# An expert-layer kernel: scatters ordered only against other experts' scatters, and an earlier transpose of the next tile's rows

## The reference, cut to what matters

```
x = x + xattn(layernorm(x), ctx, ctx, ...)      # gated linear attention, 8 heads
x = x + ffn(layernorm(x), w12, w3, gate_w)      # 8 experts, each token uses 2

scores = x @ gate_w.T                           # 8 scores for each token
topk_scores, topk_idx = top_k(scores, 2)
probs = softmax(topk_scores)
h1, h2 = split(x @ w12[e].T)                    # 512 + 512 columns, expert e
expert_out[e] = (silu(h1) * h2) @ w3[e].T       # back to 256 columns
y = sum over the 2 chosen experts of probs * expert_out
```

## Time and profile before

| what | us |
|---|---|
| median of 3 runs | 795.19 |
| the three runs | 798.36, 795.19, 791.96 |
| span of the profiled execution | 798.1 |

### The profile page before, as it was taken

The page is one execution under the profiler, slowest core; times in us unless marked ns, Lnnn a source line. Parts: engine busy times, 40 slices in busy tenths (PEclk is TensorE's granted clock), DMA queues, the critical chain, the costliest instruction groups (busy, mean ns, idle before and its releaser), DMA issues.

```text
span 798.1 us, 15053 instructions
## 1 busy us (share of the span) xinstructions
PE 662.9 (83%) x3464; PEld 486.9 (61%) x3481; DVE 463.9 (58%) x940; ACT 316.1 (40%) x704; POOL 405.0 (51%) x470
## 2 busy tenths in 40 slices
PE   3781999999999994136999999999999999999981
PEld 1330566676677663114887777777677777777760
DVE  4663477485367568992676455564555655545541
ACT  3554344353245341003555444444444444434430
POOL 2234254445335331563656666666666666566653
PEclk9996898697589695556999999999999999999995
DMA  8875655355345523401232322223223232232221
GB/s 269 283 252 168 174 146 179 116 178 173 110 133 158 173 77 107 171 7 36 41 54 40 47 47 44 50 40 47 47 42 50 42 47 47 40 47 47 41 40 21
DMA packets 70952, 76.34 MB, mean 96 GB/s; under 512 B 12366, under 2 KB 63060, under 8 KB 70932
## 3 DMA queue, kind: packets, MB, share of 16 engines
q1 hardware_dynamic: 54932, 49.86, 20.2%
q0 software_dynamic: 15712, 25.73, 17.8%
q10 hardware_dynamic: 288, 0.52, 0.2%
HBM read 53.14 MB, written 22.94 MB: 95 GB/s over the span
## 4 chain that ended last, share of the span: by engine, by line
DMA 41%; PE 30%; issue 12%; DVE 8%; POOL 3%; ACT 2%; POOLq 2%; SPq 1%; DVEq 0%; ACTq 0%
DMA out_rows<-ys,ixs 36%; PE bank L1160 8%; PE bank L1174 7%; DMA qT_scratch<-qt 3%; PE bank L1155 3%; PE bank L1157 2%; PE bank L1223 2%; POOL ixs L1076 1%; PE bank L1262 1%; PE bank L1191 1%; PE bank L1264 1%; PE bank L1263 1%; PE bank L1200 1%; DVE ohp L907 1%; DVE wabs L797 1%
## 5 line engine op out<-in xcount | busy, mean ns | idle before, releaser
L1080 POOL DMA_INDIRECT out_rows<-ys,ixs x71 | 159.5, 2246 | 72.5 <-DVE ys L959 61.8
L1262 PE MATMUL bank<-w12l,xh 128*128 x284 | 125.4, 441 | 7.0 <-issue 4.8
L959 DVE TENSOR_SCALAR ys<-bank,pc 128x256 f32<-128x256 f32 x71 | 34.4, 484 | 144.9 <-DMA out_rows<-ys,ixs 140.0
L1264 PE MATMUL bank<-w12h,xh 128*128 x284 | 113.0, 398 | 0.0
L1263 PE MATMUL bank<-w12h,xl 128*128 x284 | 112.8, 397 | 0.0
L965 DVE TENSOR_TENSOR w3l<-w,w3h 128x1024 fp32r<-128x1024 f32 x71 | 87.0, 1226 | 30.8 <-issue 29.8
L1068 POOL DMA_INDIRECT xg<-token_table,ixg x71 | 71.9, 1012 | 58.4 <-POOL ixg L1065 58.4
L1174 PEld LDWEIGHTS bank<-aug,c 128*128 128x128 f32 x512 | 78.2, 219 | 37.6 <-issue 32.8
L765 DVE SCALAR_TENSOR_TENSOR c<-bank,d 128x512 f32<-128x512 f32 x64 | 44.2, 690 | 77.0 <-PE bank L1174 69.2
L624 ACT ACTIVATE sg<-bank 128x512 f32<-128x512 f32 x71 | 42.5, 599 | 115.7 <-PE bank L1264 115.7
L1290 PE MATMUL bank<-w3l,hth 128*128 128x256 f32 x284 | 76.0, 300 | 14.0 <-issue 6.9
(11 more groups left out here) (164 smaller groups left out, 1236.5 us busy)
## 6 DMA issues: line engine op xcount, KB each, us to landing
x<-in_x SPq DMA_DIRECT2D x32, 256.0 KB, 3.0
wst<-in_w12T POOLq DMA_DIRECT2D x26, 256.0 KB, 3.6
aug<-in_ctxv SPq DMA_DIRECT2D x16, 264.0 KB, 3.0
ct<-in_ctxT SPq DMA_DIRECT2D x16, 256.0 KB, 4.5
qT_scratch<-qt SPq DMA_DIRECT2D x16, 256.0 KB, 3.8
kt<-in_ctxT SPq DMA_DIRECT2D x16, 256.0 KB
qbd<-qT_scratch SPq DMA_DIRECT2D x64, 64.0 KB
out_rows<-x SPq DMA_DIRECT2D x16, 256.0 KB, 2.2
```

Source lines behind the costliest of these rows:

```text
L1080: q.indirect_dma_start(out=out, out_offset=bass.IndirectOffsetOnAxis(ap=IXS[i][:, 0:1], axis=0), in_=YS[i][:], in_offset=None, compute_op= ...
L1262: mm(acc, XH[i][:, k, :], wl, start=(k == 0), stop=False)
L1264: ins = mm(acc, XH[i][:, k, :], wh, start=False, stop=(k == NK - 1))
```

## The change

1. **Order of the scatters.** The single semaphore `y_added` becomes two, one for even and one for odd tiles. POOL's `add(j)` waits for ys and for a new semaphore `may_add`. SP raises `may_add` once for each tile, in order: for tile j it first waits for a count of the other parity's `y_added`. The count comes from a table `clear` that DVE works out: 16*max((j-1)//2, 0), which says that scatters up to tile j-3 have landed, plus 16 when tile j has another expert than tile j-1, which says that tile j-1's has landed too. With the two YS buffers, tile j's ys implies that scatter j-2 has landed.
2. **Spare rows.** There are two sets of 128 spare rows, for even and odd tiles, so that two scatters in flight never share one. SP zeroes both (two more DMAs) and loads two small constant tables (two more DMAs, ahead of w3).
3. **Index.** The gather and the scatter read their column of `index` directly; the copies ixg and ixs and their waits go. POOL's expert stage is written out for all 71 tiles, without a loop.
4. **Order on PE and DVE.** On PE `rows(j + 1)` moves ahead of `half_up(1)`; on DVE `low(j + 1)` moves ahead of the product hd.

```
-ROWS = N + P
+ROWS = N + 2 * P
...
-                sp.dma_start(table[N:ROWS, :], zrow[:]).then_inc(zero_out, 16)
-                sp.dma_start(out[N:ROWS, :], zrow[:, 0:E]).then_inc(zero_out, 16)
+                for at in (N, N + P):
+                    sp.dma_start(table[at:at + P, :], zrow[:]).then_inc(zero_out, 16)
+                    sp.dma_start(out[at:at + P, :], zrow[:, 0:E]).then_inc(zero_out, 16)
...
+            sp.dma_start(floor16[:], floors).then_inc(slot_consts, 16)
+            sp.dma_start(spare[:], spares).then_inc(slot_consts, 16)
             sp.wait_ge(w_lo, W2 + B)
...
+            def order(j, o):
+
+                at = sp.value_load(clear[0:1, bass.ds(j, 1)], min_val=16, max_val=16 * TILES)
+                sp.wait_ge(y_added[1 - o], at)
+                sp.sem_inc(may_add, 1)
+
+            sp.wait_ge(clear_ready, 1)
+            sp.sem_inc(may_add, 1)
+            for j in range(1, 3):
+                sp.wait_ge(y_added[1 - j % 2], 16)
+                sp.sem_inc(may_add, 1)
+            order(3, 1)
+            with sp.Fori(2, TILES // 2) as it:
+                for o in range(2):
+                    order(it * 2 + o, o)
+            for j in range(TILES // 2 * 2, TILES):
+                order(j, j % 2)
...
                 st.then(v.tensor_copy(etab[:], count[:]))
+                st.then(v.tensor_tensor(turns[:, 1:], count[:, 1:], count[:, 0:TILES - 1], ALU.not_equal))
+                st.then(v.memset(clear[:, 0:1], 16))
+                dve.wait_ge(slot_consts, 32)
+                v.scalar_tensor_tensor(clear[:, 1:], turns[:, 1:], 16.0, floor16[:, 1:],
+                                       ALU.mult, ALU.add).then_inc(clear_ready, 1)
...
-            st.then(v.tensor_scalar(fil[:], bank[1][:, TILES:2 * TILES], 0.0, io[:, P:P + 1], ALU.is_equal, ALU.mult))
+            st.then(v.scalar_tensor_tensor(fil[:], bank[1][:, TILES:2 * TILES], 0.0, spare[:], ALU.is_equal, ALU.mult))
...
+                if ahead:
+                    low(j + 1, 1 - i)
                 if up:
...
                     v.tensor_tensor(HD[i][:], SG[i][:], bank[2 * i + 1][:], ALU.mult).then_inc(hd_ready, 1)
-                if ahead:
-                    low(j + 1, 1 - i)
...
-                    wait(dve, y_added, 16 * (j - 2))
+                    wait(dve, y_added[o], 8 * (j - 1 - o))
...
+            def gather(j):
+
+                x = j % NX
                 wait(pool, xt_psum, j - NX + 1)
                 wait(pool, pc_ready, j - NX + 1)
-                pool.sem_inc(pool_carrier, 1)
-                q.tensor_copy(IXG[x][:], index[:, bass.ds(j, 1)]).then_inc(ixg_ready, 1)
-                pool.wait_ge(ixg_ready, j + 1)
-                pool.sem_inc(pool_carrier, 1)
                 q.indirect_dma_start(out=XG[x][:], out_offset=None, in_=table,
-                                     in_offset=bass.IndirectOffsetOnAxis(ap=IXG[x][:, 0:1], axis=0)
+                                     in_offset=bass.IndirectOffsetOnAxis(ap=index[:, j:j + 1], axis=0)
                                      ).then_inc(xg_in[x], 16)
...
+            def add(j):
+
+                o = j % 2
                 pool.wait_ge(ys_ready, j + 1)
+                pool.wait_ge(may_add, j + 1)
+                q.indirect_dma_start(out=out, out_offset=bass.IndirectOffsetOnAxis(ap=index[:, j:j + 1], axis=0),
+                                     in_=YS[o][:], in_offset=None, compute_op=ALU.add).then_inc(y_added[o], 16)
...
+            for j in range(TILES + 1):
+                if j + NX - 1 < TILES:
+                    gather(j + NX - 1)
+                if j >= 1:
+                    add(j - 1)
...
+                if ahead:
+                    rows(j + 1, (x + 1) % NX)
                 if up:
                     half_up(1)
-                if ahead:
-                    rows(j + 1, (x + 1) % NX)
```

More of the change, by code:

```diff
@@ L77, in build @@
 def build(nc, x, ctx, ctxv, ctxT, gkq, gkk, gkv, ibias, fbias, onw, w12T, w3T, gateT, ident, identb,
-          maskT, trib, marks, iota, nums, out):
+          maskT, trib, marks, iota, nums, floors, spares, out):
     qT_dram = nc.dram_tensor("qT_scratch", (B, P, NG, S), F32).ap()
@@ L107, in build @@
         tri = sb("tri", [P, 2, P], BF16)
-        io = sb("io", [P, P + 1])
+        io = sb("io", [P, P])
         numbers = sb("numbers", [P, 2 * TOPK * NT])
@@ L112, in build @@
         etab = sb("etab", [P, TILES], I32)
+        clear = sb("clear", [P, TILES], I32)
         index = sb("index", [P, TILES], U32)
@@ L199, in build @@
         OHN = [rt(f"ohn{i}", NI * 2 * TILES, BF16) for i in range(4)]
-        fil, count = rt("fil", TILES), rt("count", TILES)
+        fil, count, turns = rt("fil", TILES), rt("count", TILES), rt("turns", TILES)
+        floor16, spare = rt("floor16", TILES), rt("spare", TILES)
         later = rt("later", TILES * (NE - 1))
@@ L213, in build @@
         PC = [sb(f"pc{i}", [P, 1], on=f) for i in range(NX)]
-        IXG = [sb(f"ixg{i}", [P, 1], U32, on=f) for i in range(NX)]
-        IXS = [sb(f"ixs{i}", [P, 1], U32, on=f) for i in range(2)]
         f.close()
@@ L255, in build @@
         hots_made, hots_ready, inverted, tables = sems("hots_made", "hots_ready", "inverted", "tables")
-        ixg_ready, ixs_ready, y_added = sems("ixg_ready", "ixs_ready", "y_added")
+        clear_ready, may_add, slot_consts = sems("clear_ready", "may_add", "slot_consts")
+        y_added = two("y_added")
         xg_in = [sem(f"xg_in_{i}") for i in range(NX)]
@@ L437, in _ @@
             sp.wait_ge(parts_out, 16 * (1 + PARTS))
-            sp.wait_ge(zero_out, 32)
+            sp.wait_ge(zero_out, 64)
             sp.wait_ge(cols_ready, 1)
@@ L1057, in _ @@
             inversion(pool, number)
-            def gather(j, x):
+            def gather(j):
+                x = j % NX
                 wait(pool, xt_psum, j - NX + 1)
                 wait(pool, pc_ready, j - NX + 1)
-                pool.sem_inc(pool_carrier, 1)
-                q.tensor_copy(IXG[x][:], index[:, bass.ds(j, 1)]).then_inc(ixg_ready, 1)
-                pool.wait_ge(ixg_ready, j + 1)
-                pool.sem_inc(pool_carrier, 1)
                 q.indirect_dma_start(out=XG[x][:], out_offset=None, in_=table,
-                                     in_offset=bass.IndirectOffsetOnAxis(ap=IXG[x][:, 0:1], axis=0)
+                                     in_offset=bass.IndirectOffsetOnAxis(ap=index[:, j:j + 1], axis=0)
                                      ).then_inc(xg_in[x], 16)
[L1072 to L1077, removed]
-                pool.wait_ge(ys_ready, j + 1)
[L1079 to L1088, removed]
+            def add(j):
+                o = j % 2
+                pool.wait_ge(ys_ready, j + 1)
+                pool.wait_ge(may_add, j + 1)
+                q.indirect_dma_start(out=out, out_offset=bass.IndirectOffsetOnAxis(ap=index[:, j:j + 1], axis=0),
+                                     in_=YS[o][:], in_offset=None, compute_op=ALU.add).then_inc(y_added[o], 16)
             pool.wait_ge(tables, 1)
@@ L1094, in _ @@
                 pool.wait_ge(row_out[i], 16 * (B // 2))
[L1095 to L1099, removed]
+            pool.wait_ge(zero_out, 64)
+            for j in range(NX - 1):
+                gather(j)
+            for j in range(TILES + 1):
[3 more added lines that the diff above has]
+                    add(j - 1)
+            for o in range(2):
+                pool.wait_ge(y_added[o], 16 * ((TILES + 1 - o) // 2))
         @block.tensor
@@ L1340 @@
         "marks": marks.astype(bf),
-        "iota": np.concatenate([np.broadcast_to(q, (P, P)), N + P + p], axis=1).astype(np.float32),
+        "iota": np.broadcast_to(q, (P, P)).astype(np.float32),
         "nums": np.stack(np.broadcast_arrays(p, 1 + np.repeat(np.arange(NT), TOPK)[None, :]),
                          axis=2).reshape(P, -1).astype(np.float32),
+        "floors": np.broadcast_to(16 * np.maximum((np.arange(TILES) - 1) // 2, 0), (P, TILES)).astype(np.float32),
+        "spares": (N + P + P * (np.arange(TILES) % 2)[None, :] + p).astype(np.float32),
     }
```

## The result

The changed kernel takes 726.57 us in the median of 4 runs (720.06 to 727.28), the kernel before 793.58 (790.37 to 798.36) in runs beside it. The ratio is 0.919, with a 95% interval of 0.910 to 0.927. All ratios here compare fast executions with fast ones, since some executions are a per cent or two slower at a lower mean granted clock; of the experiments' traces, those of e3 and e9 are of such slower ones, yet with a clock of 1.00 from 434 to 700 us. The profiled execution's span fell from 798.1 to 725.6 us.

A forecast was written before the change was run, and what follows sets the result against it. The prediction took a latency loop of scatter landings, 5.90 us a tile, as the bound. Its terms -59.3 - 0.4 - 1.1 - 8.4 + 0.5 = -68.7 brought span 798.1 to 729.4, median 726.5 us, range 718 to 741.

The forecast's parts named there:

- The stage runs at PE's pace of 4.90: Expert stage: with landings off the loop, PE sets 4.90 us a tile over tiles 1 to 69, a term of -59.3.
- rival 4: Expert stage: PE's clock falls when PE is full; at 0.75 a tile takes 6.53 us, 839 us total; chance 0.03.
- rival 2: Scatters: each still follows its predecessor's landing, 5.5 us a tile, 41 us above forecast, 768 us; chance 0.04.
- POOL's gap of 0.82 before each indirect DMA: POOL, before each gather and scatter: about 0.82 us ready but not begun, counted twice in its 4.26 us a tile.
- rival 1: POOL becomes the bound at 5.04 us a tile, costing 10 us, so 736 us; chance 0.11.
- Nearly every scatter of the new loop starts inside w3l: POOL's scatters: issued 0.9 us after ys, they meet DVE's w3l; most then took 2.36 us instead of 1.58.
- A scatter that starts first does not hold w3l up: POOL against DVE: w3l keeps its usual 1.23 us when a scatter begins before it, judged from one pair.
- rival 3: DVE: scatters that start first hold w3l up, 0.4 us beyond its slack each tile, 28 us, 754 us; chance 0.03.
- The start: Before the stage: -0.4 from reading the first gather's index in place, -1.1 from PE not waiting for xl of tile 1.
- The end: After tile 69's last matmuls: without the queue of scatters, 18.6 us to the last landing becomes 10.2, a term of -8.4.
- Added work: Start-up: two more zeroing DMAs on SP ahead of x's loads cost +0.5; DVE's added instructions 0, at most 0.6.
- The relay and the index in place: SP's waits at expert changes and tiles 1, 2: 0, at most 5.4 us; gathers reading index columns directly: 0 a tile.

The follow-up runs named there:

- e3: Changed kernel with index copies back and each scatter waiting on POOL for the previous landing: 794.62 us, ratio 1.005 to the kernel before.
- e9: e1 with the scatter's index copy and its semaphore increments back, placed ahead of the wait for the landing: 721.33 us, ratio 0.910 to the kernel before.
- e1: Changed kernel, but each scatter waits on POOL for the previous landing, SP's loop gone, index read in place: 732.98 us, ratio 0.924 to the kernel before.
- e4: Changed kernel with the flag set for every tile, so SP chains each scatter to the previous landing: 726.69 us, ratio 0.912 to the kernel before.
- e7: Changed kernel with a bare semaphore increment back before each indirect DMA on POOL, without index copies: 722.07 us, ratio 0.908 to the kernel before.
- e11: e1 with a bare semaphore increment between the wait and each indirect DMA, no index copy: 735.69 us, no ratio interval given.
- e2: Changed kernel, scatters still free, with both index copies on POOL and their waits back: 730.40 us, ratio 0.919 to the kernel before.
- e8: e1 with the scatter's index copy and its increments back, the copy behind the wait for the landing: 792.35 us, ratio 0.995 to the kernel before.
- e6: Kernel before with only the new order on PE and DVE: 795.05 us, ratio 1.000.

## Why the prediction was right, and where it was wrong

The time was forecast as 726.5 and came out at 726.57, the range and the direction held. That closeness is luck. The sum was -68.7 and the profiled execution fell by 72.5, with all four parts (stage, start, end, added work) ahead of the forecast; but the median, put 2.9 us under the profiled span, came out 1.0 above it (726.57 against 725.6), and the two errors cancel. The medians of before went from 793.04 to 796.38 between jobs.

- *The stage runs at PE's pace of 4.90.* Right: 4.894, from a stretch of ten tiles in the trace of before. The term of -59.3 measured -59.7. The clock stayed at 1.00 with PE full, so rival 4 did not occur.
- *What frees it.* Wrong in part. The prediction credited the whole term to the order of scatters and priced a chained scatter at 5.5 us a tile (rival 2, 768 us). e1 and e4 show 4.9. The step that failed is the one that carried a landing of 4.6 over to a kernel without copies. The gap did carry over (0.80 in e1, the 0.1 for the semaphore included), but the landing is 3.9 to 4.0 there, and the removal of the copies, which I put at 0, is by itself a sufficient cure.
- *POOL's gap of 0.82 before each indirect DMA.* Wrong: taken for the DMA's start-up. It is 0.30 behind another DMA and 0.28 behind ys; e7, e1 and e11 show that it belongs to a sequencer instruction between the last wait and the DMA. POOL's round, put at 4.26 to 5.04, has over 2 us of idle time; even with the copies back it keeps PE's pace (e2), so rival 1 did not occur in any run.
- *Nearly every scatter of the new loop starts inside w3l.* Wrong, for the same reason. How the hold-up works was right: e7 brings it back, and in e1 and e11 a later issue is held up less.
- *A scatter that starts first does not hold w3l up.* Right, 0.16 us ahead of w3l, which takes 1.23. The Trainium skill (page "SBUF — State Buffer", section "Who interferes with whom") says that whoever issues first gets the shared pair for the whole instruction, in a line on DVE's two-port modes, and of all cases "Issue order, not op shape, decides who blocks"; for this pair it held one way only, and rival 3 did not occur.
- *The start.* -0.4 and -1.1 against -2.96. The gather's gap fell to 0.27 (1.33 before), -1.06. PE's wait for xl, -1.08, as said. The remaining 0.8 I did not foresee. It need not come from the change: from the first gather to tile 0's mark the kernels with the new order differ by 1.1 us among themselves (13.73 to 14.83).
- *The end.* -8.4 against -9.4; the gap between ys and scatter again, 0.28 for 0.9, and an ending of the last product that took 0.64, not 1.03.
- *Added work.* +0.5 against -0.43 up to the index table. The two zeroing DMAs and DVE's three instructions cannot be seen in it, but the stretch could not show them: the first gather moves by up to 20 us from trace to trace (last section).
- *The relay and the index in place*, both put at 0: e4 (with every scatter through the relay) and the gathers' 0.99 us agree.

## What to carry to other kernels

When a loop of latency sits above an engine-bound pace, price every part of the loop against the gap between the two, here 5.90 against 4.90: any cure worth 1 us or more gives all of it, and the second cure gives nothing, so each has to be undone alone before it is credited. Put the preparation of a DMA (index copy, increments, waits for buffers) ahead of the wait that ends last, and let the DMA itself carry that wait. A gap that stands before every instance of an instruction may belong to its neighbour; look for an instance without that neighbour before carrying it over.

## What the runs showed of the hardware that was not expected

A sequencer instruction on POOL between the wait that ends last and an indirect DMA, be it a semaphore increment or a bare wait, is followed by 0.55 to 0.58 us in which nothing starts (e1's and e8's chains); an increment ahead of a scatter moved its start from 0.28 to 0.88 us behind ys (e7).

POOL is held up while DVE runs w3l, whose two inputs lie in SBUF: an index copy that reads 0.78 undisturbed read 1.03 in e2. A scatter that starts 0.1 to 1.0 us into w3l ends 1.47 us after w3l does, early or late (started 0.43 into it in e7: 2.26; 0.86 into it in e11: 1.83). One that starts 0.16 us before w3l takes 1.59, and so does one that started 0.02 us into it (changed kernel, 512.98 against 512.96), where w3l took 1.28 instead of 1.23.

The expert stage repeats to 0.24 us between kernels that share its bound (337.46 to 337.70 in eight of them), while the first gather, before which all kernels do nearly the same work, came anywhere from 348.7 us (e6) to 368.3 us (e3). Among those eight the spans differ by 14.4 us (715.9 to 730.3) and the first gather by 12.5, so most of the difference is made ahead of the stage. For the spread of one kernel's executions, 780.92 to 809.18 for the kernel before over all jobs, that is likely but not shown, since only one execution was traced.
